# Forward transforms of a Fourier layer: 24 moved columns in two blocks, and 32 stationary columns on four tiles

## Chip, core and metric

One core of a Trainium2 chip runs the whole program, in float32. The metric is the device time of one execution in microseconds.

## The reference, cut to what matters

The program computes a Fourier neural operator on 16 x 64 x 64 images that were cut into 64 pieces, a small text embedding, attention and a mixture of experts. The change is in the Fourier layers (images, 32 channels, 64 x 64 pixels):

```python
def spectral_conv(x, w1, w2):
    x_ft = jnp.fft.rfft2(x)
    out_ft = out_ft.at[:, :, :M1, :M2].set(einsum('bixy,ioxy->boxy', x_ft[:, :, :M1, :M2], w1))
    out_ft = out_ft.at[:, :, -M1:, :M2].set(einsum('bixy,ioxy->boxy', x_ft[:, :, -M1:, :M2], w2))
    return jnp.fft.irfft2(out_ft, s=(h, w))
for i in range(LAYERS):                       # 4 layers, M1 = M2 = 12
    x1 = spectral_conv(h, w1, w2)
    x2 = einsum('bchw,oc->bohw', h, conv_w[i]) + conv_b[i][None, :, None, None]
    h = layer_norm(x1 + x2)                   # over channels
    if i < LAYERS - 1: h = gelu(h)
```

Only 12 modes in x and 24 in y are kept, so both forward transforms are matrix products with small tables of cosines and sines.

## The kernel before, in words

The 64 images are worked on as 32 pairs (two images side by side in the partitions), and two pairs make a couple, one turn of a hardware loop on each engine but PE, whose loop has one pair a turn. After a stem come three passes (`layer`, s = 1 to 3), each ending in `mix`, which multiplies modes by weights; then a last pass, attention and experts. Every engine has its own written-out order, joined by semaphores. Within a pair the work goes in halves h of 8 rows, each half in two units u.

For a half the chain is: **widen** (L527, PE) adds the inverse x transform, **conv** (L544, PE) the 1x1 convolution, into the same PSUM; ACT squares (L903); DVE sums over channels (**reduce**, L1238); POOL takes the power -1/2 (L1481, about 3 us each); DVE **normalises** (L1252), then gain (L1309) and bias (L1316); ACT's **gelu** (L915) writes `hp`. From `hp`, PE makes four things for the next layer: **turn** (L591) transposes it, and ACT stores it (L929); **f1** (L615) is the forward x transform, in four blocks j of 8 channels into one PSUM bank `a_ps`, each copied to `asb` by ACT (`a_copy`, L945) before the next may start; **f2** (L629) is the forward y transform, two blocks, copied by L959. **i1** (L555) is the inverse y transform of the next pair, whose result ACT (L950) and DVE (L1321, the copy of z) bring to `zb` for widen.

PE's order for one pair g (`step` in `layer`): conv of half 0, [turn, f2, turn, f2, turn] of the pairs before, widen half 1, f1 block 0 of pair g-1, conv of half 1, then i1 in three pieces with the f1 blocks 1 to 3 between them and a turn before the last, and widen of half 0 of pair g+1. f1's first block waits for the gelu of half 1 (`hp_ready`); widen of half 0 waits for the copies of z (`zb_ready`) and for the normalise of the pair before.

DVE's order (`layer` of the vector engine) is, for half 0: normalise, gain, bias of the previous half's unit 0; reduce unit 0; the same three of unit 1; reduce unit 1. For half 1: normalise, gain, bias; reduce; normalise; reduce; gain; copy of z; bias; and once a couple the sum over the weights (L1346). POOL takes the powers in order and once a couple centres a piece of weights between them (L1491, L1493, L1497). DMAs are issued by SP and are not on this path. `keep_awake` (L503) is a matmul whose result nobody reads, where PE would else be idle at a layer's end.

In f1 the 32 stationary columns are `hp` of one channel and unit; the moved operand `d1` has 48 columns (2 images x 12 modes x real and imaginary), and the four column tiles of 32 take the two units u and, for each, the x table itself (a = 0) and the table times -i (a = 1), which the sines of the y transform need. In f2 the stationary operand is 64 columns (32 channels x real/imaginary) on two column tiles, `cy` is moved with 24 columns.

Of the kernel before, what the change touches and what calls it, by code (L numbers as in the profile page):

```python
# [25 lines left out]
PAIRS = IMGS // 2  # L26
# [58 lines left out]
def token_network(nc, t, tokens):  # L85


    with ExitStack() as ctx:
# [3 lines left out]
        def sem(name):  # L92
# [17 lines left out]
        asb = [sb(f"asb{p}", [128, 2 * KX, C, 2]) for p in range(2)]  # L110
# [10 lines left out]
              for flat in (*(tile[:].rearrange("p u c v r -> p (u c v r)") for tile in hp), asb[1][:].rearrange("p x c s -> p (x c s)"))  # L121
# [16 lines left out]
        cy = sb("cy", [128, KY])  # L138
        gbx = sb("gbx", [128, LAYERS, 2, C])
# [58 lines left out]
        def channel_ps(q):  # L198
# [6 lines left out]
        a_ps = ps[:, 7, 0:8 * TRIG * 2]  # L205
# [72 lines left out]
                 (ident, t["ident"]), (d1, t["d1"]), (cy, t["cy"])]  # L278
        late_loads = [(dyi, t["dyi"]), (ex, t["ex"]), (sgn, t["sgn"]), (side, t["side"]), (fc1, t["fc1_w"]), (fc1b, t["fc1_b"]),
                      (fc2, t["fc2_w"]), (fc2b, t["fc2_b"]), (fc3, t["fc3_w"]), (fc3b, t["fc3_b"])]  # L280
        CONSTS = 20
# [210 lines left out]
        def _(pe):  # L492
# [112 lines left out]
            def f1(s, b, g, j):  # L605
# [4 lines left out]
                pe.wait_ge(a_ready, 4 * rank(s, g) + j)  # L610
                for k in range(8):
                    for a in range(2):
                        for u in range(2):
                            row = 64 * a + 32 * u
                            last = nc.tensor.matmul(a_ps[row:row + 32, 2 * TRIG * k:2 * TRIG * k + 2 * TRIG],  # L615
                                                    hp[b][:, u, 8 * j + k].rearrange("p v r -> p (v r)"),
                                                    d1[:, a].rearrange("p x s -> p (x s)"),
                                                    start=True, stop=True, tile_position=(0, row))
                last.then_inc(a_psr, 1)

            def f2(s, b, g, m):

                if m == 0:
                    pe.wait_ge(a_ready, 4 * rank(s, g) + 4)
                    at_least(pe, x_ready, rank(s, g))
                for a in range(6):
                    for c in range(2):
                        o = KY * (6 * m + a)
                        last = nc.tensor.matmul(x_ps[64 * c:64 * c + 64, o:o + KY],  # L629
                                                asb[b][:, KX * m + 2 * a + c].rearrange("y c s -> y (c s)"),  # L630
                                                cy[:], start=True, stop=True, tile_position=(0, 64 * c))
# [62 lines left out]
            def stem():  # L694
# [19 lines left out]
                pe.sem_inc(a_psr, 3 * PAIRS)  # L714

            def layer(s):
# [7 lines left out]
                def step(g):  # L724
# [30 lines left out]
                    for j, piece in enumerate(((0, 6), (6, 11), (11, 16))):  # L755
                        if here:
                            with where_next(g):
                                i1(s, g + 1, *piece)
                        if drain:
# [1527 lines left out]
```

## Time and profile before

| | us |
|---|---|
| three runs | 3233.77, 3235.67, 3237.13 |
| median | 3235.67 |
| profiled execution, span | 3238.3 |
| PE busy | 2941.1 (91%) |
| DVE busy | 2306.9 (71%) |
| ACT busy | 2158.6 (67%) |
| POOL busy | 2115.6 (65%) |

The profiled execution has no time of its own on record beside its span, which runs from its first to its last instruction. Busy shares are of the whole span; the three layer passes lie between about 270 and 1800 us. PE's busy time includes the latency of the last matmul of each block. A float32 matmul of f1, f2, i1 and conv stands as two records in the trace, so counts of L615, L629, L555, L544 and L678 are twice the numbers of matmuls.

### The profile page before, as it was taken

To read this page: it belongs to the slowest core of one execution; us is meant where nothing else is said; L and a number is where in the kernel's file an instruction comes from. 1 tells how busy PE (TensorE), PEld (TensorE's weight loads), DVE (VectorE), ACT (ScalarE), POOL (GpSimd) and SP (SyncE) were. 2 spreads that over 40 slices of the span, in tenths; PEclk is the share of its full clock that TensorE was granted. 3 is DMA by queue.
4 is the path that set the end of the run, shared out by engine and by line. 5 is a ranking of instruction groups with operands and counts; after the bars stand their busy time and mean duration, and the time that the engine had idled before them with its cause. 6 is when DMAs were issued, how large, how long until landed. Compare 5 with 4: busy or idle time off the path is not lost. (4 is left out here: it accounts for less than half of the span.)

```text
span 3238.3 us, 190683 instructions
## 1 busy us (share of the span) xinstructions
PE 2941.1 (91%) x80542; PEld 1998.9 (62%) x80542; DVE 2306.9 (71%) x3829; ACT 2158.6 (67%) x3644; POOL 2115.6 (65%) x1147
## 2 busy tenths in 40 slices
PE   6877999997999998799999689999999969999998
PEld 4555777775777776577777434444444426777776
DVE  7766888984889886588888344444444428999996
ACT  5664777774677775477777267777777755655654
POOL 3763999993899995599999234444444425666663
PEclk9997999999999999899999789999999988999998
DMA  5764555554455554455554411111111110000000
GB/s 167 222 220 155 174 177 175 173 184 134 153 175 175 181 174 162 125 176 178 177 171 163 134 49 56 58 58 55 57 59 60 48 49 12 14 13 13 13 13 10
DMA packets 215406, 369.21 MB, mean 114 GB/s; under 512 B 116051, under 2 KB 133267, under 8 KB 215011
## 3 DMA queue, kind: packets, MB, share of 16 engines
q1 hardware_dynamic: 203602, 353.37, 34.2%
q10 hardware_dynamic: 7920, 10.03, 1.0%
q0 software_dynamic: 3744, 3.84, 0.8%
q8 instruction: 101, 1.65, 0.2%
q14 instruction: 39, 0.31, 0.0%
HBM read 209.43 MB, written 157.71 MB: 113 GB/s over the span
## 5 line engine op out<-in xcount | busy, mean ns | idle before, releaser
L1481 POOL TENSOR_TENSOR rstd<-var,mhalf 128x16 f32<-128x16 f32 x512 | 1524.3, 2993 | 689.2 <-DVE var L1238 683.7
L1238 DVE TENSOR_REDUCE var<-sq 128x16 f32<-128x528 f32 x384 | 403.5, 1052 | 87.9 <-ACT sq L903 87.3
L1252 DVE TENSOR_TENSOR zt<-ps,rstd 128x512 f32<-128x512 f32 x512 | 345.4, 684 | 77.9 <-POOL rstd L1481 71.8
L615 PEld LDWEIGHTS ps<-d,hp 128*32 128x32 f32 x24576 | 292.6, 111 | 132.0 <-ACT hp L915 98.5
L615 PE MATMUL ps<-d,hp 128*32 128x48 f32 x24576 | 345.6, 209 | 27.0 <-ACT hp L915 16.6
L544 PEld LDWEIGHTS ps<-cwl,hc 64*64 64x64 f32 x16384 | 272.8, 139 | 138.9 <-issue 132.7
L527 PE MATMUL ps<-zb,ex 48*128 48x512 f32 x1024 | 301.0, 664 | 55.8 <-DVE zt L1252 20.5
L555 PEld LDWEIGHTS ps<-dyi,gt 64*48 64x48 f32 x16384 | 230.1, 124 | 160.3 <-issue 148.7
L1074 ACT ACTIVATE a<-ps,fc1b 128x1024 f32<-128x1024 f32 x256 | 271.3, 1111 | 64.7 <-PE ps L818 64.7
L544 PE MATMUL ps<-cwl,hc 64*64 64x64 f32 x16384 | 308.5, 226 | 0.0
L903 ACT ACTIVATE sq<-ps 128x512 f32<-128x512 f32 x384 | 218.9, 598 | 129.5 <-PE ps L544 118.4
L555 PE MATMUL ps<-dyi,gt 64*48 64x32 f32 x16384 | 272.2, 210 | 34.1 <-ACT gt L969 14.4
L945 ACT COPY asb<-ps 128x384 f32<-128x384 f32 x384 | 191.5, 499 | 165.7 <-PE ps L615 165.7
L1238 DVE TENSOR_REDUCE var<-sql 128x16 f32<-128x528 f32 x128 | 141.6, 1108 | 208.3 <-ACT sql L903 208.3
L915 ACT ACTIVATE hp<-zt 128x512 f32<-128x512 f32 x384 | 231.9, 628 | 80.8 <-DVE zt L1316 80.8
L1309 DVE TENSOR_TENSOR zt<-zt,gbx 128x512 f32<-128x512 f32 x384 | 275.7, 718 | 10.2
L591 PE MATMUL ps<-ident,hp 128*128 128x128 f32 x1536 | 273.9, 301 | 6.7 <-ACT ho L929 4.9
L1316 DVE TENSOR_TENSOR zt<-zt,gbx 128x512 f32<-128x512 f32 x384 | 265.0, 690 | 10.3
L834 PE MATMUL ps<-a,fc 128*64 128x512 f32 x1024 | 254.0, 616 | 3.5 <-ACT a L1074 3.5
L2124 POOL TENSOR_TENSOR sm<-sm,mx 128x952 f32<-128x952 f32 x96 | 176.1, 1835 | 96.7 <-DVE mx L2025 96.7
L929 ACT COPY ho<-ps 128x512 f32<-128x512 f32 x384 | 223.5, 582 | 12.0 <-PE ps L591 4.3
L591 PEld LDWEIGHTS ps<-ident,hp 128*128 128x128 f32 x1536 | 202.9, 196 | 29.0 <-ACT ho L929 8.0
(198 smaller groups left out, 4999.7 us busy)
## 6 DMA issues: line engine op xcount, KB each, us to landing
h_scratch<-ho SPq DMA_DIRECT2D x256, 512.0 KB
hc<-h_scratch SPq DMA_DIRECT2D x256, 512.0 KB, 3.9
wsb<-in_w SPq DMA_DIRECT2D x64, 288.0 KB
gin<-g_scratch SPq DMA_DIRECT2D x252, 72.0 KB
gin<-g_scratch SPq DMA_DIRECT2D x504, 36.0 KB
g_scratch<-hp ACTq DMA_DIRECT2D x32, 192.0 KB, 4.8
g_scratch<-hp SPq DMA_DIRECT2D x32, 192.0 KB, 3.9
tokens<-wsb SPq DMA_DIRECT2D x256, 4.0 KB
```

The lines of the kernel that those rows point to most:

```text
L527: nc.tensor.matmul(main_ps(s, h, u), ex[k], zb[b][k, h, :], start=True, stop=False, skip_group_check=True, tile_position=(64 * u, 0))
L544: last = nc.tensor.matmul(main_ps(s, h, u)[64 * m:64 * m + 64, r:512:8], hc[b][k, 8 * h + r, 64 * m:64 * m + 64], cwl[k], start=False, sto ...
L555: last = nc.tensor.matmul(z[c][64 * u:64 * u + 2 * TRIG, 32 * col:32 * col + 32], gt[b][rows, k].rearrange("k n s a -> k (n s a)"), dyi[ro ...
L591: last = nc.tensor.transpose(t_mid[:, 128 * a:128 * a + 128], src, ident[:])
L615: last = nc.tensor.matmul(a_ps[row:row + 32, 2 * TRIG * k:2 * TRIG * k + 2 * TRIG], hp[b][:, u, 8 * j + k].rearrange("p v r -> p (v r)"), ...
L834: last = nc.tensor.matmul(f2_ps[64 * v:64 * v + 64, u, :], fc2[:], a1[:, 2 * u + v, :], start=True, stop=True, tile_position=(0, 64 * v))
L1074: nc.scalar.activation(a1[:, 2 * u:2 * u + 2, :], f1_ps[:, 2 * u:2 * u + 2, :], ACT.Gelu, bias=fc1b[:]).then_inc(a1_ready, 1)
L1238: nc.vector.tensor_reduce(dst, src, axis=AX.X, op=ALU.add).then_inc(var_ready, 1)
L1252: nc.vector.tensor_tensor(by_px(zt[h][:, u]), by_px(main_ps(s, h, u)), scale, ALU.mult).then_inc(norm_ready, 1)
L1309: nc.vector.tensor_tensor(z, z, channels(s, 0).unsqueeze(2).to_broadcast([128, C, 16]), ALU.mult).then_inc(gain_ready, 1)
L1316: nc.vector.tensor_tensor(z, z, channels(s, 1).unsqueeze(2).to_broadcast([128, C, 16]), ALU.add).then_inc(zt_ready, 1)
L1481: nc.gpsimd.tensor_tensor(rstd[u][:], var[u][:], mhalf[:], ALU.pow).then_inc(rstd_ready, 1)
```

## The change

f1 is now two blocks of 16 channels. The moved operand has 24 columns (2 images x 12 modes): the column tile `part` takes the real or the imaginary part of the table, each once, where before both parts stood in each of two tiles. Real and imaginary parts are joined in f2 instead, which has one more table for it (`dy`). A block's PSUM result has the same 128 x 384 size, holds 16 channels and is copied by ACT in memory order into `asb`, now one buffer laid out channel by channel. f2 takes 32 stationary columns (channels, 96 bytes apart) on four column tiles, two for the real and two for the imaginary part, so it has 24 matmuls a block where it had 12, each with 24 moved columns. In PE's order the three pieces of i1 are one, followed by turn and the second f1 block; ACT's order loses two copies. Semaphore counts follow. The weights' rows are laid out real channels first, and with them `f0x`, `sgn` and `stem_gb`; `f0x` is centred in two groups instead of one. Two tables `dx` and `dy` are loaded at the start; `d1` and `cy` stay for the stem. `gs` buffers that lay in `asb` get a tile of their own.

```diff
...
-        asb = [sb(f"asb{p}", [128, 2 * KX, C, 2]) for p in range(2)]
+        asb = sb("asb", [128, C, 2 * KX])
+        grow = sb("grow", [128, 2 * 768])
...
-              for flat in (*(tile[:].rearrange("p u c v r -> p (u c v r)") for tile in hp), asb[1][:].rearrange("p x c s -> p (x c s)"))
+              for flat in (*(tile[:].rearrange("p u c v r -> p (u c v r)") for tile in hp), grow[:])
...
+        dx = sb("dx", [128, 2, 2 * KX])
+        dy = sb("dy", [128, 2, KY])
...
-        a_ps = ps[:, 7, 0:8 * TRIG * 2]
+        a_ps = ps[:, 7, 0:CH * 2 * KX]
...
-                 (ident, t["ident"]), (d1, t["d1"]), (cy, t["cy"])]
+                 (ident, t["ident"]), (d1, t["d1"]), (cy, t["cy"]), (dx, t["dx"]), (dy, t["dy"])]
...
-        CONSTS = 20
+        CONSTS = 21
...
-                pe.wait_ge(a_ready, 4 * rank(s, g) + j)
-                for k in range(8):
-                    for a in range(2):
+                pe.wait_ge(a_ready, 2 * rank(s, g) + j)
+                for k in range(CH):
+                    for part in range(2):
...
-                            row = 64 * a + 32 * u
-                            last = nc.tensor.matmul(a_ps[row:row + 32, 2 * TRIG * k:2 * TRIG * k + 2 * TRIG],
-                                                    hp[b][:, u, 8 * j + k].rearrange("p v r -> p (v r)"),
-                                                    d1[:, a].rearrange("p x s -> p (x s)"),
+                            row = 64 * part + 32 * u
+                            last = nc.tensor.matmul(a_ps[row:row + 32, 2 * KX * k:2 * KX * k + 2 * KX],
+                                                    hp[b][:, u, CH * j + k].rearrange("p v r -> p (v r)"), dx[:, part],
...
             def f2(s, b, g, m):
...
-                    pe.wait_ge(a_ready, 4 * rank(s, g) + 4)
+                    pe.wait_ge(a_ready, 2 * rank(s, g) + 2)
...
-                        o = KY * (6 * m + a)
-                        last = nc.tensor.matmul(x_ps[64 * c:64 * c + 64, o:o + KY],
-                                                asb[b][:, KX * m + 2 * a + c].rearrange("y c s -> y (c s)"),
-                                                cy[:], start=True, stop=True, tile_position=(0, 64 * c))
+                        for part in range(2):
+                            o, row = KY * (6 * m + a), 64 * c + 32 * part
+                            last = nc.tensor.matmul(x_ps[row:row + 32, o:o + KY], asb[:, :, KX * m + 2 * a + c],
+                                                    dy[:, part], start=True, stop=True, tile_position=(0, row))
...
-                pe.sem_inc(a_psr, 3 * PAIRS)
+                pe.sem_inc(a_psr, PAIRS)
...
             def layer(s):
...
-                    for j, piece in enumerate(((0, 6), (6, 11), (11, 16))):
-                        if here:
-                            with where_next(g):
-                                i1(s, g + 1, *piece)
-                        if drain:
-                            keep_awake(z_mid[0], 128, 2)
-                        if old and j == 2:
-                            turn(s, 0, g - 1, 1, 0)
-                        if old:
-                            f1(s, 0, g - 1, j + 1)
+                    if here:
+                        with where_next(g):
+                            i1(s, g + 1, 0, CH)
+                    if drain:
+                        keep_awake(z_mid[0], 128, 3)
+                    if old:
+                        turn(s, 0, g - 1, 1, 0)
+                        f1(s, 0, g - 1, 1)
...
-                    act.wait_ge(a_psr, 4 * rank(s, g))
+                    act.wait_ge(a_psr, 2 * rank(s, g))
...
-            def a_copy(s, b, g, j):
-                act.wait_ge(a_psr, 4 * rank(s, g) + j + 1)
-                nc.scalar.copy(asb[b][:, :, 8 * j:8 * j + 8, :].rearrange("p x g s -> p g x s"),
-                               a_ps.rearrange("p (g x s) -> p g x s", g=8, s=2)).then_inc(a_ready, 1)
+            def a_copy(s, g, j):
+                act.wait_ge(a_psr, 2 * rank(s, g) + j + 1)
+                nc.scalar.copy(asb[:, CH * j:CH * j + CH].rearrange("p c x -> p (c x)"), a_ps).then_inc(a_ready, 1)
...
             def z_copy(s, g):
...
-                act.sem_inc(a_ready, 3 * PAIRS)
+                act.sem_inc(a_ready, PAIRS)
...
             def layer(s):
...
                 def odd(i, p):
...
-                        a_copy(s, 0, old[0], 0)
+                        a_copy(s, old[0], 0)
...
-                    if old:
-                        a_copy(s, 0, old[0], 1)
-                        a_copy(s, 0, old[0], 2)
...
-                        a_copy(s, 0, old[0], 3)
+                        a_copy(s, old[0], 1)
...
-                     (f0x[:].rearrange("p w (a c b) -> p (w a) b c", a=2, b=2), f0xm[:], [128, 4, 2, C])]
+                     (f0x[:, 0].rearrange("p (a c b) -> p a b c", a=2, b=2), f0xm[:, 0:2], [128, 2, 2, C]),
+                     (f0x[:, 1].rearrange("p (m c) -> p m c", c=C), f0xm[:, 2:4].rearrange("p a b -> p (a b)"), [128, 4, C])]
...
-    w = np.empty((LAYERS, 2, C, 2, 6, KY, 2, C), np.float32)
-    w[:, :, :, 0, ..., 0, :], w[:, :, :, 0, ..., 1, :] = wr, wi
-    w[:, :, :, 1, ..., 0, :], w[:, :, :, 1, ..., 1, :] = wi, wr
+    w = np.empty((LAYERS, 2, 2, C, 6, KY, 2, C), np.float32)
+    w[:, :, 0, ..., 0, :], w[:, :, 0, ..., 1, :] = wr, wi
+    w[:, :, 1, ..., 0, :], w[:, :, 1, ..., 1, :] = wi, wr
...
-    f0x = np.zeros((128, 2, 2, C, 2), np.float32)
+    f0x, f0m = np.zeros((128, 2, C, 2), np.float32), np.zeros((128, 2, 2, C), np.float32)
...
-                    f0x[[32 * n + 8 * a + 2 * k + b, 64 + 32 * n + 8 * a + 2 * k + b], 0, a, :, b] = f4[k]
-                    f0x[64 * n + 32 * a + 2 * k + b, 1, a, :, b] = f4[k]
-    out["fc0x"] = f0x.reshape(128, 2, 4 * C)
+                    f0x[[32 * n + 8 * a + 2 * k + b, 64 + 32 * n + 8 * a + 2 * k + b], a, :, b] = f4[k]
+                    f0m[64 * n + 32 * a + 2 * k + b, a, b] = f4[k]
+    out["fc0x"] = np.stack([f0x.reshape(128, 4 * C), f0m.reshape(128, 4 * C)], axis=1)
...
-    out["stem_gb"] = np.stack([np.tile(np.repeat(sg, 2), 2), np.tile(np.repeat(sb_, 2), 2), np.tile(np.repeat(sg, 2), 2),
-                               np.concatenate([np.stack([sb_, zero[0:C]], axis=1).reshape(64), zero])], axis=1)
+    out["stem_gb"] = np.stack([np.tile(np.repeat(sg, 2), 2), np.tile(np.repeat(sb_, 2), 2), np.tile(sg, 4),
+                               np.concatenate([sb_, zero[0:C], zero])], axis=1)
...
+    out["dx"] = d1[:, :, 0].reshape(128, TRIG, 2).transpose(0, 2, 1)
...
+    out["dy"] = np.stack([out["cy"], np.concatenate([by_y(-np.sin(ty)), by_y(np.cos(ty))])], axis=1)
...
-    out["sgn"] = np.tile([1.0, -1.0], 2 * C)[:, None]
+    out["sgn"] = np.tile(np.repeat([1.0, -1.0], C), 2)[:, None]
```

## Rows read from the trace of the kernel before

**Rows 1.** The page: length of the profiled execution.

```profile
span 3238.3 us, 190683 instructions
```

**Rows 2.** Windows: stretch, us, PE, PEld, DVE, ACT, POOL busy, clock, DMA, GB/s.

```profile
900.00:1100.00 200.00, 193.16 (x8067) 153.59 (x8058) 178.84 (x244) 151.15 (x279) 182.24 (x77) 1.00 0.55 177
...
150.00:300.00 150.00, 115.27 (x2929) 77.95 (x2933) 95.37 (x271) 82.72 (x183) 80.08 (x79) 0.86 0.61 195
```

**Rows 3.** Timeline of one couple: start us, us, engine line op, count [idle <-releaser].

```profile
907.89 6.25 POOL L1481 TENSOR_TENSOR rstd<-var,mhalf 128x16 f32<-128x16 f32 x2
...
913.45 1.04 DVE L1238 TENSOR_REDUCE var<-sq 128x16 f32<-128x528 f32 x1
```

**Rows 4.** Timeline of the same couple, from the DVE copy of z to the next power.

```profile
916.58 0.69 DVE L1321 COPY zb<-ps 112x512 f32<-112x512 f32 x1
...
917.32 1.13 PE L527 MATMUL ps<-zb,ex 48*128 48x512 f32 x4 [0.26 <-DVE zb L1321]
...
918.38 1.16 PE L544 MATMUL ps<-cwl,hc 64*64 64x64 f32 x64
...
919.69 0.60 ACT L903 ACTIVATE sq<-ps 128x512 f32<-128x512 f32 x1 [1.03 <-PE ps L544]
...
920.40 1.05 DVE L1238 TENSOR_REDUCE var<-sq 128x16 f32<-128x528 f32 x1 [0.49 <-ACT sq L903]
...
921.38 0.68 DVE L1252 TENSOR_TENSOR zt<-ps,rstd 128x512 f32<-128x512 f32 x1
...
923.54 0.63 ACT L915 ACTIVATE hp<-zt 128x512 f32<-128x512 f32 x1 [0.46 <-DVE zt L1316]
...
924.22 0.89 PE L615 MATMUL ps<-d,hp 128*32 128x48 f32 x64
...
925.04 1.16 PE L544 MATMUL ps<-cwl,hc 64*64 64x64 f32 x64
...
926.36 1.09 ACT L903 ACTIVATE sq<-ps 128x512 f32<-128x512 f32 x2 [0.16 <-PE ps L544]
...
926.99 1.06 DVE L1238 TENSOR_REDUCE var<-sq 128x16 f32<-128x528 f32 x1 [0.29 <-ACT sq L903]
...
928.13 6.05 POOL L1481 TENSOR_TENSOR rstd<-var,mhalf 128x16 f32<-128x16 f32 x2 [0.69 <-DVE var L1238]
...
936.72 6.25 POOL L1481 TENSOR_TENSOR rstd<-var,mhalf 128x16 f32<-128x16 f32 x2
```

**Rows 5.** Timeline of the same couple: its earlier first f1 block, and conv.

```profile
909.92 0.89 PE L615 MATMUL ps<-d,hp 128*32 128x48 f32 x64 [0.31 <-ACT hp L915]
...
910.74 1.16 PE L544 MATMUL ps<-cwl,hc 64*64 64x64 f32 x64
```

**Rows 6.** Timeline: f2_x in the stem (8 stationary columns on four tiles).

```profile
33.80 0.65 PE L678 MATMUL ps<-cy,hp 128*8 128x24 f32 x48
```

**Rows 7.** Timeline: f2, a third of i1 and a turn in the layers.

```profile
920.13 0.89 PE L629 MATMUL ps<-cy,asb 128*64 128x24 f32 x24
...
927.74 0.65 PE L555 MATMUL ps<-dyi,gt 64*48 64x32 f32 x40
...
929.82 0.72 PE L591 MATMUL ps<-ident,hp 128*128 128x128 f32 x4
```

**Rows 8.** Timeline of PE at the end of a layer: f1, two keep-awake matmuls, f2.

```profile
750.70 0.89 PE L615 MATMUL ps<-d,hp 128*32 128x48 f32 x64 [0.81 <-ACT hp L915]
...
751.52 0.71 PE L503 MATMUL ps<-ident 128*128 128x128 f32 x4
...
757.39 1.59 PE L629 MATMUL ps<-cy,asb 128*64 128x24 f32 x48
```

**Rows 9.** Timeline of the start: the last load of constants, a reduction of the constants.

```profile
5.75 0.43 SPq L342 DMA_DIRECT2D cy<-in_cy  x1
...
10.40 0.41 DVE L1196 TENSOR_REDUCE f0xm<-f0x 128x8 f32<-128x256 f32 x1
```

**Rows 10.** Timeline: a conv at the granted clock's lower level.

```profile
278.37 1.98 PE L544 MATMUL ps<-cwl,hc 64*64 64x64 f32 x64
```

## The prediction

> **What bounds the kernel now.** I began with the page for the length of the execution [rows 1], then took the windows: in the steady part of the layers PE is busy 193 of 200 us, POOL 182 and DVE 179, at the full granted clock [rows 2]. Three engines near their limit, and PE first: this view alone would say that any PE work saved comes back as time. But a busy PE in this profile includes each matmul's latency, so I went to the timeline and asked of every engine which instruction it waited for. The steady state repeats exactly: the power (L1481) at 907.89 has its like at 936.72 [rows 3, 4], one couple of pairs later, 28.83 us. Walking back from 936.72 gives a closed loop, each step the last releaser of the next:
>
> - POOL power 907.89, then DVE's normalise, gain and bias, then the reduction at 913.45: 5.56 [rows 3]. DVE was ready for it only then; conv had long delivered.
> - From that reduction DVE goes in its fixed order to the copy of z, 916.58 to 917.27; widen starts on it at 917.32, conv of the next pair's first half (C0) at 918.38 [rows 4]: 4.93.
> - C0, the square, the reduction at 920.40: 2.02. DVE sat idle 0.49 for it.
> - The previous half's normalise at 921.38 stands behind that reduction in DVE's order; then gain, bias, gelu at 923.54, and f1's first block (F0) at 924.22: 3.82.
> - F0 to the conv of the second half (C1) at 925.04: 0.82. PE executes in order, and conv is queued behind the whole first f1 block.
> - C1, square, reduction at 926.99: 1.95, DVE idle 0.29; the power at 928.13: 1.14, POOL idle 0.69.
> - Two powers and three instructions that centre weights on POOL, to 936.72: 8.59.
>
> 5.56 + 4.93 + 2.02 + 3.82 + 0.82 + 1.95 + 1.14 + 8.59 = 28.83. So the time of a couple is a loop of latencies through four engines, and PE stands on it with little: widen, two convs and **one first f1 block**. The f2 blocks and turns run between C0 and F0 but end before gelu does; i1 and the later f1 blocks run under the DVE copy and the power.
>
> **The change, part by part.** A block of f1 had 64 records (32 matmuls, two records each), 0.89 us busy [rows 5], of which about 0.2 is the last one's own latency: 0.69/63 = 11.0 ns a record. For the new form (32 stationary, 24 moved columns, four tiles) the trace has no row, and two near ones bound it: f2_x, 24 moved columns and 8 stationary on four tiles, (0.65 - 0.18)/47 = 10 ns [rows 6], and f1 itself with 48 moved columns, 11 ns. So halving the moved columns buys about 1 ns in 11, not half. The Trainium skill (TensorEngine Tiling, Instruction Overhead) says that a matmul with one free column has the latency of one with 60; by that rule nothing at all is bought, the block stays at 11 ns, and the sum below would be some 5 us higher. The row of f2_x speaks for a slightly better value.
>
> *First f1 block.* It now holds 16 channels, 128 records. A block's step to the next instruction is 0.82 [rows 4], its records 0.69, so 0.13 for the change of shape. New: 127 x 10 ns + 0.13 = 1.40, or 127 x 11 ns + 0.13 = 1.53. I take 1.42, near the row with the same 24 moved columns. On the loop 0.82 becomes 1.42: **+0.60 a couple** (bounds +0.58 and +0.71). It counts once a couple: for the other pair F0 to C1 is the same 0.82 [rows 5], but C1 + 1.95 = 912.69 while DVE was not ready until 913.45, a slack of 0.76 that swallows it.
>
> *Saved on PE.* f1: 4 x 0.82 = 3.28 becomes 2 x 1.42 = 2.84. f2: a block of 24 records takes (0.89 - 0.22)/23 = 29 ns each [rows 7]; 48 records on four tiles at 10 ns make 0.60 for 0.80, twice. i1 in one piece instead of three saves two changes of shape, 0.26. Together 1.1 us a pair. All of it lies between C0 and F0, where gelu sets the end, or between C1 and widen, where the copy of z does: in the pair at 907.89 the copy is 3.83 after the reduction in DVE's own order, and the change does not touch that order. Cost on the loop: nothing, and if that cover were gone the kernel would be faster. The strided stationary read of f2 I price at nothing: turn's stationary is strided too and its four instructions take 0.72 [rows 7] in cover.
>
> *ACT.* Two copies of 384 columns a pair fewer, some 1.0 us. ACT is busy 151 of 200 us [rows 2] and is on the loop only with squares and gelu, each of which waited for PE or DVE (0.16, 0.46) [rows 4]. Nothing. The first copy ends near F0 + 2.1, before the squares at C1 + 1.3 = F0 + 2.7, so the wait added for its semaphore queues nothing behind it.
>
> *Semaphores, buffers.* The copy of the second block is needed only by f2 a step later; gelu of the next half waits for it, and comes earlier than before. No cost.
>
> *Ends of layers.* There the f1 blocks stand one behind the other: F0 at 750.70, f2 at 757.39, f2 itself 1.59 [rows 8]. New: 1.42, three keep-awake matmuls (two took 0.7, so 1.0), turn 0.65, 1.42, turn 0.65, and 0.15 for the copy: 5.3 for 6.7; f2 96 records, 1.15 for 1.59. About -1.8 a layer, **-5.4** in all.
>
> *Start.* Two more loads at 0.47 each ahead of the constants (the last is issued at 5.75) and one more reduction, scaling and subtraction, each at most the 0.41 of the large reduction, while that one becomes smaller [rows 9]: 0.9 + 0.5, **+1.4**, with nothing to hide them.
>
> **The sum.** 15 steady couples in each of three layers: 45 x 0.60 = +27.0; -5.4; +1.4: **+23.0 us**. The profiled span is 3238.3; the record has no separate time for that execution, and the median of the runs, 3235.67, is 2.6 lower. I put the difference on the median: 3258.7, say 3259. With the bounds of the block: 45 x 0.58 to 0.71 gives 3258 to 3264. A measurement of this kernel can tell about 0.2%, 6.5 us.
>
> **The rivals.**
> 1. *PE is the bound after all (faster), chance 0.15.* Its place is PE between C0 and the next widen. For it: 193 of 200 us. Against: idle times with a DVE releaser at widen and an ACT releaser at F0 [rows 4, 5]. It decides if gelu and the copy of z are waiting for PE through a step I missed. If the waits at C0, F0 and C1 all vanished, DVE's idle of 0.49 and 0.29 in these rows is what comes back, near 0.75 a couple: 45 x 0.75 = 34, less 4 for the ends: 3198. All 1.1 a pair, 2.2 a couple, would be 3235.7 - 99 - 4 = 3133; POOL's 182 of 200 leaves just room for that, so I hold 3198 for its likelier size.
> 2. *The longer block is absorbed (no change), 0.12.* If F0 comes earlier by the 0.4 that f2 saves, or DVE gains slack, the 0.60 is hidden and the ends remain: 3235.7 - 4 = 3232. Against it: F0 at 924.22 is 0.05 behind the end of gelu at 924.17 [rows 4].
> 3. *The granted clock falls (slower by more), 0.12.* After the change PE is done with the last f1 block about 1.6 us before widen may start in the pair at 907.89 (C1 + 1.2 + 1.6 + 0.65 + 1.42 against C1 + 2.7 + 3.9). In the steady layers it was busy 193 of 200 us at a full clock; in the stem 115 of 150, at 0.86 [rows 2]. At the lower level of 1.2 GHz conv takes 1.98 instead of 1.16 [rows 10]: 0.8 a couple if one conv on the loop meets it, 45 x 0.8 = 36 more: 3295. The Trainium skill (TensorE: Matmul & The Clock Gate, The HAM clock gate) has half rate as the default which activity lifts; the rows of the stem agree, the layers of before never put it to the test.
>
> **How the numbers follow.** Forecast 0.61, rivals 0.15, 0.12 and 0.12. Slower: 0.61 + 0.12 = 0.73; same 0.12; faster 0.15. The range leaves out the first rival and most of the third, and reaches down over the second: 3230 to 3285. The forecast's own range is 3250 to 3270, with 2 to 3 us a layer for the cold first couple, whose doubled block I have not counted.
>
> **What would show it.** Right: couples of 29.4 us between powers; F0 to C1 1.4 and PE waiting over 1 us at widen for the copy of z; POOL's idle before the second half's power of the second pair 1.2 to 1.3 instead of 0.69; f2 blocks under 0.7 us; ACT idle up by 1 us a pair. Wrong: couples under 28.8, or the same couple with F0 earlier against C0 than 5.84, or half-clock stretches inside the layers. If a block of 128 records took clearly under 1.2 us, the term of +0.60 fails first.

## The result and the profile after

The changed kernel takes **3332.93 us** (median of four runs, 3327.53 to 3336.55) where the kernel before, on the same chip, takes 3234.93: a ratio of 1.0298, with an interval of 1.0283 to 1.0312. It is 98 us slower; forecast were 3259, and a range up to 3285.

The page of the changed kernel: its span, and what the engines did in it.

```profile
span 3325.7 us, 199490 instructions
...
PE 2890.7 (87%) x85132; PEld 1963.9 (59%) x85132; DVE 2312.1 (70%) x3832; ACT 2079.4 (63%) x3452; POOL 2128.3 (64%) x1147
```

The span answers to [rows 1] and is 87.4 us longer. The profiled execution, 3327.53, is the shortest of the four, and that of before was a little longer than its median, so about 10 of the 98 us lie in this choice. What follows is worked out in the spans.

The same window as in [rows 2], with the same columns (stretch, us, busy of PE, PEld, DVE, ACT and POOL, clock, DMA, GB/s):

```profile
900.00:1100.00 200.00, 176.34 (x8272) 141.76 (x8272) 170.06 (x231) 132.33 (x237) 172.93 (x74) 0.96 0.52 168
```

PE is busy 176 us for 193, DVE 170 for 179, POOL 173 for 182. In the same length of time every engine is busy less; all wait more. And the granted clock is 0.96 where it was 1.00. The lengths of the stretches come from the powers on POOL, as in [rows 3, 4]. From the first power of a pass over the images to its last, the three layers took 462.6, 462.4 and 462.5 us before, and 490.8, 493.6 and 493.3 now: **+90.2 us**. All that lies outside them sums to -2.8.

The timeline of one couple at the full clock, which answers to [rows 3, 4] (start us, us, engine, line, operation, count, idle time and its releaser; f1 is L618 now, f2 L632, widen L530, conv L547, the copy of z L1318, the reduction L1235, the gain L1306, the bias L1313, the power L1478):

```profile
907.03 6.08 POOL L1478 TENSOR_TENSOR rstd<-var,mhalf 128x16 f32<-128x16 f32 x2 [1.14 <-DVE var L1235]
...
914.65 0.73 DVE L1306 TENSOR_TENSOR zt<-zt,gbx 128x512 f32<-128x512 f32 x1
...
915.03 0.88 POOL L1494 TENSOR_TENSOR wsb<-wsb,sgn 128x288 f32 x1 [0.19 <-POOL wsb L1490]
...
915.42 1.04 DVE L1313 TENSOR_TENSOR zt<-zt,gbx 128x512 f32<-128x512 f32 x1
...
915.87 6.24 POOL L1478 TENSOR_TENSOR rstd<-var,mhalf 128x16 f32<-128x16 f32 x2
...
921.42 1.05 DVE L1235 TENSOR_REDUCE var<-sq 128x16 f32<-128x528 f32 x1
...
924.54 0.68 DVE L1318 COPY zb<-ps 112x512 f32<-112x512 f32 x1
...
925.27 1.13 PE L530 MATMUL ps<-zb,ex 48*128 48x512 f32 x4 [2.10 <-DVE zb L1318]
...
926.34 1.16 PE L547 MATMUL ps<-cwl,hc 64*64 64x64 f32 x64
...
928.09 0.97 PE L632 MATMUL ps<-dy,asb 128*32 128x24 f32 x48
...
928.36 1.06 DVE L1235 TENSOR_REDUCE var<-sq 128x16 f32<-128x528 f32 x1 [0.49 <-ACT sq L903]
...
931.50 0.63 ACT L915 ACTIVATE hp<-zt 128x512 f32<-128x512 f32 x1 [0.41 <-DVE zt L1313]
...
932.26 1.28 PE L618 MATMUL ps<-dx,hp 128*32 128x24 f32 x128
...
933.47 1.16 PE L547 MATMUL ps<-cwl,hc 64*64 64x64 f32 x64
...
935.42 1.05 DVE L1235 TENSOR_REDUCE var<-sq 128x16 f32<-128x528 f32 x1 [0.75 <-POOL rstd L1478]
...
936.55 6.09 POOL L1478 TENSOR_TENSOR rstd<-var,mhalf 128x16 f32<-128x16 f32 x2 [1.14 <-DVE var L1235]
```

The loop of before closes here too, over the same eight steps: power 907.03, two powers and the centring to 915.87 (8.84), to the reduction at 921.42 (5.55), to conv C0 at 926.34 (4.92), to the reduction at 928.36 (2.02), to F0 at 932.26 (3.90), to conv C1 at 933.47 (1.21), to the reduction at 935.42 (1.95), to the power at 936.55 (1.13): 29.52 us for 28.83. Three steps grew: the first f1 block by 0.39, the centring on POOL by 0.25, the step to F0 by 0.08.

But few couples are so. Most take between 30.2 and 31.3. PE's timeline in such a one:

```profile
371.30 1.28 PE L618 MATMUL ps<-dx,hp 128*32 128x24 f32 x128
374.69 1.32 PE L530 MATMUL ps<-zb,ex 48*128 48x512 f32 x4 [2.10 <-DVE zb L1318]
375.93 1.98 PE L547 MATMUL ps<-cwl,hc 64*64 64x64 f32 x64
```

and two windows of it, from F0 to widen and behind the start of conv, with the columns of above:

```profile
371.30:374.60 3.30, 1.28 (x129) 1.17 (x128) 3.30 (x6) 1.66 (x4) 2.86 (x2) 1.00 0.81 198
376.00:378.50 2.50, 2.50 (x68) 2.38 (x68) 1.25 (x2) 0.44 (x1) 1.99 (x1) 0.50 0.01 5
```

PE has done its last f1 block and stands 2.10 us before widen for DVE's copy of z. Then the granted clock is 0.50, that is 1.2 GHz of its 2.4: widen takes 1.32 us instead of 1.13 and conv 1.98 instead of 1.16, both on the loop. A layer has 16 couples; called steady here are the 14 behind the first that have another one behind them. In them the trace has 11, 11 and 10 such stretches in the three layers, 32 for 42 couples, and before it had none. The wait alone does not decide: each of these couples has one of 2.10 to 2.12 us, the couple at 907.03 too (at 925.27), which kept the full clock.

### The profile page after: what moved, and what is told of

Its sections match the earlier page's. It is cut to its first block and busy times, and to the rows that moved or that the text cites. A ratio compares the mean times of both kernels' runs of the same rounds, so it can differ in the third digit from the quotient of the medians.

```text
span 3325.7 us, 199490 instructions
## 1 busy us (share of the span) xinstructions
PE 2890.7 (87%) x85132; PEld 1963.9 (59%) x85132; DVE 2312.1 (70%) x3832; ACT 2079.4 (63%) x3452; POOL 2128.3 (64%) x1147
## 5 line engine op out<-in xcount | busy, mean ns | idle before, releaser
L1478 POOL TENSOR_TENSOR rstd<-var,mhalf 128x16 f32<-128x16 f32 x512 | 1526.4, 2999 | 762.6 <-DVE var L1235 757.0
L1235 DVE TENSOR_REDUCE var<-sq 128x16 f32<-128x528 f32 x384 | 403.1, 1050 | 140.8 <-ACT sq L903 126.5
L530 PE MATMUL ps<-zb,ex 48*128 48x512 f32 x1024 | 315.4, 694 | 173.9 <-DVE zb L1318 142.3
L547 PEld LDWEIGHTS ps<-cwl,hc 64*64 64x64 f32 x16384 | 297.9, 150 | 148.1 <-issue 144.8
L915 ACT ACTIVATE hp<-zt 128x512 f32<-128x512 f32 x384 | 242.1, 631 | 181.5 <-DVE zt L1313 180.7
L547 PE MATMUL ps<-cwl,hc 64*64 64x64 f32 x16384 | 335.1, 238 | 0.0
L558 PEld LDWEIGHTS ps<-dyi,gt 64*48 64x48 f32 x16384 | 215.8, 125 | 152.0 <-issue 151.8
L618 PEld LDWEIGHTS ps<-dx,hp 128*32 128x32 f32 x24576 | 232.2, 111 | 120.2 <-issue 109.0
L594 PE MATMUL ps<-ident,hp 128*128 128x128 f32 x1536 | 288.9, 314 | 13.2 <-ACT ho L929 10.8
L1313 DVE TENSOR_TENSOR zt<-zt,gbx 128x512 f32<-128x512 f32 x384 | 280.0, 729 | 10.3
L1235 DVE TENSOR_REDUCE var<-sql 128x16 f32<-128x528 f32 x128 | 141.5, 1107 | 207.0 <-ACT sql L903 207.0
L618 PE MATMUL ps<-dx,hp 128*32 128x24 f32 x24576 | 252.9, 193 | 28.2 <-ACT hp L915 18.9
L558 PE MATMUL ps<-dyi,gt 64*48 64x32 f32 x16384 | 238.0, 210 | 40.4 <-ACT gt L968 15.0
L1306 DVE TENSOR_TENSOR zt<-zt,gbx 128x512 f32<-128x512 f32 x384 | 265.8, 692 | 10.2
L530 PEld LDWEIGHTS ps<-zb,ex 48*128 48x128 f32 x1024 | 81.4, 194 | 249.5 <-DVE zb L1318 148.8
```

The lines of the kernel that those rows point to most:

```text
L530: nc.tensor.matmul(main_ps(s, h, u), ex[k], zb[b][k, h, :], start=True, stop=False, skip_group_check=True, tile_position=(64 * u, 0))
L547: last = nc.tensor.matmul(main_ps(s, h, u)[64 * m:64 * m + 64, r:512:8], hc[b][k, 8 * h + r, 64 * m:64 * m + 64], cwl[k], start=False, sto ...
L558: last = nc.tensor.matmul(z[c][64 * u:64 * u + 2 * TRIG, 32 * col:32 * col + 32], gt[b][rows, k].rearrange("k n s a -> k (n s a)"), dyi[ro ...
L594: last = nc.tensor.transpose(t_mid[:, 128 * a:128 * a + 128], src, ident[:])
L618: last = nc.tensor.matmul(a_ps[row:row + 32, 2 * KX * k:2 * KX * k + 2 * KX], hp[b][:, u, CH * j + k].rearrange("p v r -> p (v r)"), dx[:, ...
L1235: nc.vector.tensor_reduce(dst, src, axis=AX.X, op=ALU.add).then_inc(var_ready, 1)
```

## The experiments

Two theories stood against each other after this. **Clock:** most of the loss is the granted clock, set off by PE's wait before widen; the rest is the longer block. **Latency:** the half-clock stretches are met by slack, and the time is lost on the loop. The couple figures below are medians of the distances between powers eight apart on POOL, over all steady couples of the three layers (for kernels with half-clock stretches, over those without one); the stretches are counted in the steady couples.

| kernel | couple at the full clock | half-clock stretches, by layer | median us | ratio to before |
|---|---|---|---|---|
| before | 28.82 | 0, 0, 0 | 3235 to 3238 | 1 |
| after | 29.52 | 11, 11, 10 | 3332.93 | 1.0298 (1.0283 to 1.0312) |
| e1, after with filler | 29.54 | 0, 0, 0 | 3285.42 | 1.0144 (1.0127 to 1.0161) |
| e2, before, longer first block | 30.14 | 0, 0, 0 | 3310.20 | 1.0218 (1.0201 to 1.0235) |
| e3, after, f1 behind conv | 28.46 | 8, 7, 8 | 3263.24 | 1.0079 (1.0062 to 1.0096) |
| e4, e3 with filler | 28.47 | 0, 0, 0 | 3236.71 | 0.9998 (0.9988 to 1.0009) |
| e5, half of f1 behind conv, filler | 28.78 | 0, 0, 0 | 3253.90 | 1.0052 (1.0036 to 1.0067) |
| e6, before, f1 behind conv | 29.22 | 0, 0, 0 | 3264.38 | 1.0078 (1.0060 to 1.0096) |
| e7, e1 with less filler | 29.53 | 11, 13, 10 | 3323.27 | 1.0268 (1.0245 to 1.0290) |
| e8, e4, more filler at the edge | 28.46 | 0, 0, 0 | 3245.89 | 1.0028 (1.0016 to 1.0040) |
| e9, e4, a little more at the edge | 28.47 | 0, 0, 0 | 3232.98 | 0.9988 (0.9976 to 1.0000) |
| e10, e4, channels side by side | 28.47 | 0, 0, 0 | 3240.95 | 1.0011 (1.0001 to 1.0022) |

**e1, filler matmuls in the wait.** Three matmuls that nobody reads, put into PE's wait before the first widen of a step; nothing else changes.

```diff
                 pe.wait_ge(norm_ready, 2 * q if is_last(s) else 2 * q - 2)
+                if h == 0 and not is_last(s) and not isinstance(g, int):
+                    keep_awake(main_ps(s, 0, 0), 128, 3)
```

> The changed kernel with three matmuls that nobody reads (128 columns each, about 0.3 us each) put where PE waits for the copy of z ahead of widen; the output is unchanged. Theory A (the granted clock): of the 98 us lost, about two thirds are half-clock stretches that begin in this wait and fall on widen and conv, which are on the loop. Then the half-clock stretches inside the layers vanish, every couple takes 29.5 us instead of up to 31.3, and the time is 3333 - 60 = 3265 to 3280. Theory B (latency alone): the half-clock stretches fall where PE has slack and cost little; the couples are long because the first f1 block stands before conv. Then the time stays above 3315, whatever the clock does.

Its window, PE's timeline before widen, and two powers one couple apart:

```profile
900.00:1100.00 200.00, 186.81 (x8754) 150.90 (x8752) 174.31 (x236) 135.02 (x245) 178.81 (x74) 1.00 0.54 173
```

```profile
900.34 6.24 POOL L1480 TENSOR_TENSOR rstd<-var,mhalf 128x16 f32<-128x16 f32 x2
...
907.69 0.93 PE L506 MATMUL ps<-ident 128*128 128x128 f32 x6
909.75 1.13 PE L532 MATMUL ps<-zb,ex 48*128 48x512 f32 x4 [1.13 <-DVE zb L1320]
...
929.86 6.25 POOL L1480 TENSOR_TENSOR rstd<-var,mhalf 128x16 f32<-128x16 f32 x2
```

The clock in the steady couples is full again, no stretch is left in them, and the time falls by 47.5 us against the changed kernel: the half-clock stretches cost that, half of the loss. The clock theory had expected two thirds, and 3280 as its upper end. The couples are 29.54, within 0.03 of the undisturbed ones of after, so the filler itself costs next to nothing. The other half stays.

**e7, less filler.** The same line with one filler matmul instead of three.

> The changed kernel with one filler matmul in PE's wait instead of three. If the half clock needs most of the wait to stay empty, one matmul (about 0.3 of 2.1 us) leaves some half-clock stretches and the time lies between 3285 and 3333. If any activity in the wait is enough: no such stretch in the steady layers, and 3285 as with three. In either case full-clock couples stay at 29.5.

PE's timeline before widen (L506 the filler, L532 widen, L549 conv):

```profile
435.19 0.48 PE L506 MATMUL ps<-ident 128*128 128x128 f32 x2
437.25 1.14 PE L532 MATMUL ps<-zb,ex 48*128 48x512 f32 x4 [1.57 <-DVE zb L1320]
438.31 1.98 PE L549 MATMUL ps<-cwl,hc 64*64 64x64 f32 x64
```

A wait of 1.57 us is left, conv still meets the half clock, and 34 stretches are there, no fewer than in after. So one filler is not enough in this kernel, three are; the 1.13 us of wait that e1 leaves are harmless.

**e2, only the first block made longer.** In the kernel before, the first f1 block runs its eight channels twice.

```diff
                 pe.wait_ge(a_ready, 4 * rank(s, g) + j)
-                for k in range(8):
+                for k in (*range(8), *(range(8) if j == 0 else ())):
```

> The kernel before, with the 32 matmuls of each first f1 block issued twice (64 more records at 11 ns, 0.70 us, same result). If the first f1 block stands on the loop once a couple, as the prediction has it, the couple goes from 28.82 to about 29.5 and the time up by 45 x 0.70 = 32 us, to 3265 to 3270, with the clock full. If the block is covered: within 5 us of before. If PE is the bound, both pairs pay: 29.5 + 0.7 = 30.2 a couple and 3297.

```profile
910.45 6.24 POOL L1481 TENSOR_TENSOR rstd<-var,mhalf 128x16 f32<-128x16 f32 x2
...
912.48 1.57 PE L615 MATMUL ps<-d,hp 128*32 128x48 f32 x128 [0.28 <-ACT hp L915]
...
940.60 6.25 POOL L1481 TENSOR_TENSOR rstd<-var,mhalf 128x16 f32<-128x16 f32 x2
```

The block is 1.57 us busy for 0.89 [rows 4], its step longer by 0.70, and the couple grows from 28.82 to 30.14, by 1.32. The loop crosses one such block a couple and would give 29.5; the third case of the expectation, both blocks paid, had 30.2. PE runs two of them, 1.40 us, and 30.14 - 1.40 = 28.74. So PE's own round in the kernel before was, by this estimate, 0.1 us below the loop that set its time, or 0.4 if the 0.28 us that PE still waits for gelu once a couple are taken off as well: the second bound was near, and it decides here. The time is 13 us above that case; the first couples of the layers take 10.8 of it. The window of 193 busy us in 200 [rows 2] had hinted at the second bound; I gave it 0.15. For the changed kernel it decides nothing, since PE there has 2.10 and 1.09 us of waits in a couple.

**e3 and e4, f1 behind conv.** In the changed kernel conv of the second half goes ahead of the first f1 block, and on ACT its squares ahead of the block's copy; e4 adds the filler of e1.

```diff
@@ PE, layer
-                    if old:
-                        f1(s, 0, g - 1, 0)
                     if here:
                         conv(s, 0, g, 1)
+                    if old:
+                        f1(s, 0, g - 1, 0)
@@ ACT, layer
-                    if old:
-                        a_copy(s, old[0], 0)
                     if here:
                         square(s, here[0], 1, 0)
                         square(s, here[0], 1, 1)
+                    if old:
+                        a_copy(s, old[0], 0)
```

> The changed kernel with the conv of half 1 issued ahead of the first f1 block on PE, and its squares ahead of the first copy on ACT. The loop no longer holds an f1 block (1.2 us). If the loop is as read, the couple at full clock falls from 29.5 to about 28.8, where DVE's order and POOL set it; half-clock stretches may stay, since PE idles as much. Time 3240 to 3300. If instead PE's waits come from elsewhere: above 3320.

> Both edits together. Theory A and the loop together: no half-clock stretches in the steady layers and couples of 28.1 to 28.8 us: 3205 to 3245, at or below the kernel before. If the two causes are the same one, it is no better than the better of the two alone.

POOL's timeline in e4: the powers around a centring (L1496 answers to L1494 of after), and the one a couple later:

```profile
897.00 6.04 POOL L1480 TENSOR_TENSOR rstd<-var,mhalf 128x16 f32<-128x16 f32 x2 [0.29 <-DVE var L1237]
...
904.96 0.67 POOL L1496 TENSOR_TENSOR wsb<-wsb,sgn 128x288 f32 x1 [0.19 <-POOL wsb L1492]
905.59 6.26 POOL L1480 TENSOR_TENSOR rstd<-var,mhalf 128x16 f32<-128x16 f32 x2
...
934.06 6.25 POOL L1480 TENSOR_TENSOR rstd<-var,mhalf 128x16 f32<-128x16 f32 x2
```

With the block off the loop the couple is 28.47, by 1.07 shorter than e1 and by 0.35 shorter than before. The first f1 block, which conv stands behind, is thus what the rest of the loss can be bought back with. But not all of the 1.07 was lost by the change: the block stood on the loop before too, with 0.82 of its 1.21 us, and 0.21 is the last multiplication of the centring, which takes 0.67 us here and 0.88 in after and e1. e3 shows that the clock is a matter of its own, since it has the short couples and still 23 stretches and 26.5 us more than e4. With both removed the changed kernel runs as fast as the kernel before, and no faster (0.9988 to 1.0009): of the 42 x 0.35 = 14.7 us that its steady couples save, the first couples of the layers (36.3, 38.7 and 39.2 us against 34.5, 34.3 and 34.5) take 10.8 back.

**e5, half of the block.** As e4, but eight of the sixteen channels stay ahead of conv: the size of the block on the loop of before, with the new form.

```diff
-                        f1(s, 0, g - 1, 0)
+                        f1(s, 0, g - 1, 0, 0, 8)
                     if here:
                         conv(s, 0, g, 1)
+                    if old:
+                        f1(s, 0, g - 1, 0, 8, CH)
```

> The changed kernel with the filler of the first experiment, and the first f1 block cut around conv: 8 of its 16 channels before the conv of half 1, 8 behind it (its copy on ACT behind the squares). If each record in front of conv costs its own 8.6 ns once a couple, the couple lies between the two measured ends, 29.55 with 128 records in front and 28.47 with none: the block in front is 64 x 8.6 ns + 0.13 = 0.68 instead of 1.20, so 29.0 us and about 3260. If only the order of conv and block matters and not the size, 29.5 and 3285.

```profile
917.36 6.25 POOL L1484 TENSOR_TENSOR rstd<-var,mhalf 128x16 f32<-128x16 f32 x2
...
946.16 6.25 POOL L1484 TENSOR_TENSOR rstd<-var,mhalf 128x16 f32<-128x16 f32 x2
```

28.78 us, a little under the 29.0 expected and between 28.47 and 29.54: the size of the block ahead of conv counts, and not only the order. It does not count evenly. The first 64 records taken away give 0.76 (0.55 by 8.6 ns each, and 0.21 from the centring, whose multiplication is at 0.67 here), the next 64 only 0.31, so by then something else is near the bound.

**e6, f1 behind conv in the kernel before.** The edit of e3 made in the kernel with four blocks. It asks whether the order is good by itself, or only with two blocks.

> The kernel before with the conv of half 1 ahead of the first f1 block (and the squares ahead of its copy on ACT), nothing else. The loop loses the block's 0.82, but PE has little room left in this kernel. If the loop bound it: couples of 28.1 to 28.5 and 3215 to 3228. If PE is as near a bound as the experiment with doubled blocks suggests (its couple rose by 1.3 where the loop alone gave 0.7): 28.7 to 28.9, within 5 us of before.

```profile
914.23 0.89 PE L615 MATMUL ps<-d,hp 128*32 128x48 f32 x64 [0.23 <-ACT asb L945]
...
923.86 6.25 POOL L1481 TENSOR_TENSOR rstd<-var,mhalf 128x16 f32<-128x16 f32 x2
...
953.08 6.25 POOL L1481 TENSOR_TENSOR rstd<-var,mhalf 128x16 f32<-128x16 f32 x2
```

Neither case had this: the couple grows to 29.22. With four blocks behind conv, PE waits between them for ACT's copy of the one before (0.23 here, 0.30 in the other pair) and in this couple for no other engine, and PE's round was close below the loop already (e2). The same order costs 0.40 us a couple with four blocks and gains 1.07 with two (e1 to e4). So the two larger blocks do have a worth, which the change as it stands doesn't use.

**e8 and e9, the edges.** Since e4 loses in the first couples of the layers, its first step got more filler where three matmuls of 512 columns stand: ten in e8, six in e9.

```diff
-keep_awake(ps[:, 7, :], 512, 3)
+keep_awake(ps[:, 7, :], 512, 10)
```

> The changed kernel with conv ahead of f1, the filler, and ten keep-awake matmuls instead of three in a pass's first step, where PE waits at half clock. Steady couples 28.47 as before this edit. If the first couple of a pass (36 to 39 us here, 34.5 in the kernel before) is long because of the clock, it falls by 2 to 4 us a pass and the time to 3225 to 3232, below the kernel before. If it is long for PE's own issue waits, which stand in the trace there, it stays at 3237.

> As the last experiment, with six keep-awake matmuls instead of ten in a pass's first step. In the trace with ten they run at half clock for 7 us past the point where widen could start, so ten are too many; six last about 3 us less. If the first couple is long by the clock and ten merely overshot: first couples of 34 to 36 us and 3225 to 3232, faster than the kernel before. If the first couple hangs on PE's issue waits (2 to 4 us a pass in the trace) and on chance: 3232 to 3245, no change.

PE's timeline at the first step of e8:

```profile
290.00 7.13 PE L506 MATMUL ps<-ident 128*128 128x512 f32 x16 [2.16 <-issue]
```

Ten overshoot: the filler runs to 297.1 with widen right behind it, the first couples are 42.9, 40.6 and 37.0, together 6.5 us more than in e4, and the time grows by 9 us. With six they are 42.4, 36.0 and 39.6, still 3.8 more, and the ratio is 0.9988 (0.9976 to 1.0000), which this measurement can't tell from e4 or from the kernel before. The first couples are not bought back this way.

**e10, the stride of f2's stationary.** As e4, with `asb` laid out so that the 32 channels which f2 loads lie side by side; the copy on ACT writes them strided instead.

```diff
-        asb = sb("asb", [128, C, 2 * KX])
+        asb = sb("asb", [128, 2 * KX, C])
-                                                    asb[:, :, KX * m + 2 * a + c],
+                                                    asb[:, KX * m + 2 * a + c],
-nc.scalar.copy(asb[:, CH * j:CH * j + CH].rearrange("p c x -> p (c x)"), a_ps)
+nc.scalar.copy(asb[:, :, CH * j:CH * j + CH].rearrange("p x c -> p c x"),
+               a_ps.rearrange("p (c x) -> p c x", x=2 * KX))
```

> As the fourth experiment (conv ahead of f1, filler), with the tile asb laid out mode by mode instead of channel by channel, so that ACT's copy writes with a stride and f2 reads its 32 stationary columns side by side. In the changed kernel a block of f2 (48 records) is busy 0.97 us, 16.6 ns a record, where the prediction had 10. If the 96-byte stride of the stationary read costs this, the block falls to about 0.65 and PE gains 0.6 us a pair; if not, it stays at 0.97 and another property of four tiles with 24 moved columns is the reason. The couple is set by DVE and POOL there, so 28.45 to 28.5 and 3230 to 3240 either way.

The groups of instructions in a stretch of the layers, first e4, then e10 (f2's weight loads and matmuls, the copy on ACT; busy us, mean ns of one, idle before):

```profile
L634 PEld LDWEIGHTS ps<-dy,asb 128*32 128x32 f32 x2688 | 48.7, 162 | 6.8
...
L634 PE MATMUL ps<-dy,asb 128*32 128x24 f32 x2688 | 54.6, 224 | 0.0
...
L947 ACT COPY asb<-ps 128x384 f32<-128x384 f32 x56 | 27.0, 482 | 17.8 <-PE ps L620 17.8
```

```profile
L634 PEld LDWEIGHTS ps<-dy,asb 128*32 128x32 f32 x2688 | 28.7, 111 | 6.8
...
L634 PE MATMUL ps<-dy,asb 128*32 128x24 f32 x2688 | 34.5, 192 | 0.0
...
L947 ACT COPY asb<-ps 128x384 f32<-128x384 f32 x57 | 49.2, 863 | 16.8 <-PE ps L620 16.8
```

A weight load takes 162 ns from channels 96 bytes apart and 111 ns from adjacent ones; a block of 48 records falls from 0.97 to 0.62 us, which is 16.6 and 9.1 ns a record with the last one's latency of 0.19 taken off. Over the stretch loads and matmuls both shrink by 20 us. ACT pays: 863 ns a copy for 482. The couple stays at 28.47 and the time does not improve: PE's wait for the copy of z grows instead, from 0.19 in e4's couple at 905.59 to 0.85 in one of e10 (at 921.59).

## Why the prediction was wrong

**The step that failed** is the price of PE's new wait before widen. The sum itself made one of 1.6 us and put it at nothing; the granted clock in it was left to a rival of 0.12. In the spans the loss is 87.4 us, where 23.0 were forecast: the half-clock stretches are 47.9 where nothing stood, the first couples 9.4 where nothing stood, the ends of the layers +1.4 for -5.4, the loop 32.8 for 27.0 (30.3 in the steady couples, 2.5 in the last couples of the three layers), start and tail -4.2 for +1.4.

**The loop** was read rightly, and so were the direction and most steps of before: the eight steps close again in the changed kernel, and e3 to e5 show that the first f1 block on it is what conv waits for.

**The block** was priced at +0.60 from 10 ns a record, between bounds of 0.58 and 0.71. It measured 1.21 for 0.82, +0.39. Its records take (1.28 - 0.19)/127 = 8.6 ns: 24 moved columns for 48 bought 2.4 ns of 11, not 1. The bounds were the two nearest rows, but the one with 24 columns was f2_x, with 48 records of another shape; I took it as the lower end, and it wasn't. POOL's idle time in the other pair, forecast at 1.2 to 1.3, follows with 1.14. The Trainium skill (TensorEngine Tiling, Instruction Overhead) gives a matmul with one free column the latency of one with 60, so that 24 columns for 48 would buy nothing; the trace does not agree, by these 2.4 ns.

**The first two rivals** fell. Work on PE was saved and the couples grew all the same, so PE is not the bound of the changed kernel; and with a full clock (e1) the longer block is not absorbed.

**The other growth of the loop** was not in the sum. The centring's last multiplication on POOL takes 0.88 us for 0.67. In the kernel before it had a DVE instruction beside it too:

```profile
907.26 0.67 POOL L1497 TENSOR_TENSOR wsb<-wsb,sgn 128x288 f32 x1 [0.19 <-POOL wsb L1493]
907.52 0.95 DVE L1309 TENSOR_TENSOR zt<-zt,gbx 128x512 f32<-128x512 f32 x1
```

There POOL began first, kept its 0.67 us, and the DVE gain took 0.95 for the usual 0.69. Now a gain is under way when POOL begins (914.65 to 915.38), POOL takes 0.88, and the bias behind the gain 1.04 (915.42). In e4 POOL begins first again, it takes 0.67 and the step 8.59. With +0.08 to F0 this makes 0.72 a couple by the steps and 0.69 by the powers, some 30 us in the 42 steady couples; forecast were 27 in 45. Two errors, one each way, made that term look good. That the two engines stand in each other's way at SBUF, and that the order of the starts decides which one loses, is argued from these overlaps; no run tried it by itself. The Trainium skill (SBUF — State Buffer, Who interferes with whom) has a DVE instruction with two SBUF inputs contend with a GpSimd instruction that reads SBUF; the trace agrees in that the DVE instruction beside this multiplication is longer in both kernels, and in after the multiplication as well.

**The granted clock** was the third rival, at a chance of 0.12 and 3295. The mechanism was put right: PE done early, idle before widen, conv at 1.98. The wait is 2.10 us where I had 1.6, because both blocks are shorter and the copy of z no earlier. What went wrong is the weight: the row of the stem had this clock at 0.86 where PE was busy 115 of 150 us [rows 2], the couple of before had no wait of PE above 0.31 us [rows 4, 5], and the sum itself made one of 1.6. That spoke for a much higher chance. Its price was too low as well, 0.8 a couple from conv alone: widen grows by 0.19 as well, the turn behind conv takes 1.12 for 0.71, and couples with a stretch reach 31.3, up to 1.8 more than the others. Against e1 the three layers lost 47.9 us, 1.5 for each of the 32 stretches. The Trainium skill (TensorE: Matmul & The Clock Gate, HAM oscillation — how this bites in real kernels) tells of a kernel that falls to half rate again and again because PE waits between its bursts; the trace agrees, with 32 stretches behind such waits, and e1 shows it by filling the wait.

**The first couples** of the layers were mentioned with 2 to 3 us each and left out of the sum. They are 36.7, 38.8 and 37.3 us in after and 37.2, 38.3 and 37.2 in e1, for 34.5, 34.3 and 34.5: 9.4 us in both. They are not at the full clock in any kernel: its mean in them is 0.85 before, and 0.81, 0.74 and 0.73 in after, and PE also waits for nothing that the profile shows (at 310.93 below). Which of the two makes them longer stays open, and it is not a mark of the new form alone: e2 and e6, with four blocks, have 36.9 to 38.7 and 38.3 to 39.1.

**The ends of layers** were to save 5.4. The stretches between a layer's last power and the next one's first changed by +0.3, -0.5 and +1.6, together +1.4. PE's timeline there, which answers to [rows 8], after the one wait of the first step:

```profile
310.93 0.29 PE L558 MATMUL ps<-dyi,gt 64*48 64x32 f32 x1 [3.76 <-issue]
...
779.87 1.24 PE L618 MATMUL ps<-dx,hp 128*32 128x24 f32 x124 [0.19 <-ACT hp L915]
783.53 0.25 PE L618 MATMUL ps<-dx,hp 128*32 128x24 f32 x4 [2.41 <-issue]
...
787.18 0.42 PE L618 MATMUL ps<-dx,hp 128*32 128x24 f32 x15 [0.46 <-issue]
...
788.58 1.75 PE L632 MATMUL ps<-dy,asb 128*32 128x24 f32 x96
```

From F0 to f2 it takes 8.71 us, where 5.3 were forecast and 6.69 were before. Two waits of 2.41 and 0.46 us, released by nothing that the profile shows, make most of the 3.4; and f2 takes 1.75 for a forecast 1.15, since its stationary is strided.

**f2** was priced at a gain of 0.20 a block and its stride at nothing, by the row of the turn. Its step is 0.91 (928.09 to 929.00) for 0.82: a loss. e10 shows the stride to be the cause. It cost nothing in the steady layers, where PE waits, and about 0.6 us at each end.

**ACT, semaphores and buffers** were priced at nothing, and no row of the loop shows them. **The start** was +1.4; the first power comes 0.8 later, which says little: it lies between 280.0 and 284.9 us in the twelve profiled executions. Behind the layers, from the last pass's first power, the execution is 5.0 us shorter; this stretch lies between 1391.6 and 1397.8 us in the twelve, and between 1391.7 and 1396.6 in the three with four blocks alone, so it can't be put down to the change.

The sum in the spans: 47.9 of clock in the steady couples, 42.2 that e1 has as well (30.3 in the steady couples, 9.4 in the first ones, 2.5 in the last), +0.8 + 1.4 - 5.0: 87.3 of 87.4.

**e6** was a miss of its own: its expectation asked how near PE's round was and gave 28.7 to 28.9 us for it, but had no term for PE's waits for ACT's copies between the four blocks, and the couple was 29.22.

## What to carry to other kernels

If a change shortens work on PE that is not on the loop, it makes a wait there, and the sum has to ask what the clock does in it: here 2.1 us before one widen a couple cost half of the loss, and three filler matmuls took that half back. Larger blocks of a transform belong behind the matmul that others wait for, not ahead of it; with the filler the same change then costs nothing here. And with a loop of latencies found, work out the second bound too: PE's round was within 0.1 to 0.4 us of it.

## What the runs showed of the hardware

- Waits of PE of 2.10 us, one in each of 42 couples, came with 32 stretches of the granted clock at half; one filler matmul and 1.57 us of wait with 34; three filler matmuls and 1.13 us with none.
- f32 matmuls with 32 stationary columns on four column tiles: 11.0 ns a record with 48 moved columns, 8.6 ns with 24.
- A stationary of 32 f32 columns 96 bytes apart takes 162 ns to load, adjacent 111 ns, and the matmuls take 16.6 and 9.1 ns a record. The turn's stationary, also strided, takes 0.72 us for four instructions in both kernels and gave no hint of it [rows 7].
- In the first turn of a layer, and at its end, PE waited up to 3.76 us for nothing that the profile shows (at 310.93 above). That it waited for its instructions would fit: the profile's queue 8, of the kind "instruction", moves a packet between 307.2 and 311 us and none between 340 and 740, where no such wait stands. The first couple of the kernel before has as many of them, six. No run tried it.
- Beside the same multiplication on POOL, a DVE instruction of 0.69 us took 0.95 where POOL had begun first; where a DVE instruction was under way, POOL took 0.88 us for 0.67.
